# A Mamba-2 macaron block on 8 cores: the order of the in_proj columns, and the place of the SiLU gate

## The reference

```
x = x + 0.5 * ffn(layernorm(x))            # 1024 -> 4096 -> 1024, sin/cos transform and relu
x = x + attn(layernorm(x))                 # attn: its own layernorm, mamba2, residual, MLP with gelu
x = x + 0.5 * ffn(layernorm(x))
```

```python
zxbcdt = x @ in_proj_w.T                   # z: 2048, xBC: 2048 + 64 + 64, dt: 32
z, xBC, dt = split(zxbcdt)                 # dt = softplus(dt + dt_bias)
xBC = silu(conv1d_width_4(xBC) + conv_b)
# 32 heads of 64, state 64:  h = h*exp(dt*A) + dt*x*B ;  y = h.C + D*x
y = y * silu(z)                            # the gate
y = y * rsqrt(mean(y*y) + eps) * norm_w    # RMS norm over 2048
out = y @ out_proj_w.T
```

## Time and profile before

| | |
|---|---|
| time, median of 3 runs | 8764.91 us (8673.56, 8764.91, 8771.05) |
| the profiled execution | 8673.56 us |
| span of its slowest core (core 0) | 8671.6 us; the others 8571.8 to 8661.1 |
| busy share of the span | PE 61%, DVE 50%, ACT 22%, POOL 1% |
| mean DMA rate | 75 GB/s |

### The profile page before, as it was taken

How to read it: one execution, slowest core, us unless ns; L and a number is a source line. 1 busy time by engine, 2 the same in 40 slices (tenths; PEclk the granted TensorE clock), 3 DMA queues, 4 the chain that set the end, 5 groups by cost and what they waited for, 6 DMA issues and landing times.

```text
span 8671.6 us, 106339 instructions; the slowest of 8 cores (8571.8 to 8671.6 us)
## 1 busy us (share of the span) xinstructions
PE 5279.0 (61%) x22944; PEld 2303.2 (27%) x22944; DVE 4339.4 (50%) x11279; ACT 1874.3 (22%) x3876; POOL 60.1 (1%) x117
## 2 busy tenths in 40 slices
PE   0049999944544544445445344454468989888888
PEld 0013333322212222222222122222223434333333
DVE  2035656556456465565564655655632313556564
ACT  0022323221121211211212112112121222323232
POOL 2000000000000000000000000000000000000000
PEclk7568788865655755656557556566579999999999
DMA  9963333310100200101002001011024444343434
GB/s 171 204 155 116 107 117 117 110 50 1 40 29 1 67 1 9 59 1 37 31 1 67 1 7 61 1 35 33 1 81 136 136 134 139 112 136 117 137 123 129
DMA packets 191424, 652.87 MB, mean 75 GB/s; under 512 B 21472, under 2 KB 46176, under 8 KB 179552
## 3 DMA queue, kind: packets, MB, share of 16 engines
q1 hardware_dynamic: 174672, 590.41, 21.6%
q0 software_dynamic: 16176, 55.66, 4.4%
HBM read 629.56 MB, written 72.09 MB: 81 GB/s over the span
## 4 chain that ended last, share of the span: by engine, by line
PE 43%; DVE 31%; issue 13%; DMA 8%; ACT 3%; DVEq 2%; ACTq 0%; SPq 0%; POOL 0%; POOLq 0%
PE ps L252 42%; DVE arena L588 4%; DVE arena L583 4%; DVE arena L786 3%; DVE hstate L1045 3%; DVE arena L592 3%; DVE arena L939 3%; DVEq L92 2%; DVE arena L1124 2%; DMA arena<-wffn 2%; DMA arena<-wm 1%; DVE arena L995 1%; DMA cffn<-arena 1%; ACT arena L1109 1%; PE p L259 1%
## 5 line engine op out<-in xcount | busy, mean ns | idle before, releaser
L252 PE MATMUL ps<-arena,wk 128*128 128x512 f16 x15552 | 3710.1, 400 | 1004.9 <-DMA wk<-cffn 511.2
L252 PEld LDWEIGHTS ps<-arena,wk 128*128 128x128 f16 x15552 | 1554.5, 102 | 3152.7 <-issue 1880.0
L252 PE MATMUL ps<-arena 128*64 128x128 f16 (+1 forms) x1568 | 475.5, 303 | 1226.0 <-DVE arena L939 1162.7
L1061 ACT ACTIVATE arena<-arena 128x128 f32<-128x128 f32 x1024 | 316.6, 309 | 2197.4 <-DVE arena L995 2197.4
L583 DVE SCALAR_TENSOR_TENSOR arena<-arena,prm,ps 128x512 f32<-128x512 f32 x512 | 382.2, 746 | 647.4 <-ACT arena L581 559.1
L252 PEld LDWEIGHTS ps<-arena 128*64 128x64 f16 (+1 forms) x1568 | 198.3, 126 | 1467.8 <-issue 1404.4
L995 DVE TENSOR_SCALAR arena<-ps,arena 128x128 f32<-128x128 f32 x1024 | 358.9, 350 | 291.9 <-PE ps L252 217.3
L1004 DVE TENSOR_TENSOR arena<-arena,ps 64x128 f16<-64x128 f16 x1024 | 286.4, 280 | 387.0 <-PE ps L252 295.3
L578 ACT ACTIVATE arena<-ps,prm 128x512 f32<-128x512 f32 x512 | 352.0, 687 | 526.0 <-DVE arena L588 501.7
L252 PE MATMUL ps<-arena,ones 128*128 128x128 f16 (+1 forms) x832 | 250.3, 341 | 267.3 <-ACT arena L1109 141.4
L588 DVE SCALAR_TENSOR_TENSOR arena<-arena,prm 128x512 f32<-128x512 f32 x512 | 384.2, 750 | 54.7 <-DVE arena L583 1.8
(11 more groups left out here) (121 smaller groups left out, 3841.7 us busy)
## 6 DMA issues: line engine op xcount, KB each, us to landing
wk<-cffn SPq DMA_DIRECT2D x512, 512.0 KB, 4.0
wk<-cm SPq DMA_DIRECT2D x256, 512.0 KB, 3.7
wk<-cip SPq DMA_DIRECT2D x136, 512.0 KB, 3.6
wk<-cop SPq DMA_DIRECT2D x64, 512.0 KB, 3.8
arena<-wffn POOLq DMA_DIRECT2D x16, 1024.0 KB, 16.0
cffn<-arena SPq DMA_DIRECT2D x16, 1024.0 KB, 9.3
arena<-wm POOLq DMA_DIRECT2D x16, 1024.0 KB, 13.0
cm<-arena SPq DMA_DIRECT2D x16, 1024.0 KB, 6.9
```

What stands on the lines that cost most here:

```text
L252: e.matmul(a, l, r, start=st, stop=sp, tile_position=tp),
L1061: sD[s] = B.E("s", lambda e, s=s: e.activation(Dex[s % 2], e1[s % 2], AF.Exp), waits=[(s_v, ve1[s])], inc=s_s)
```

## The change

The in_proj loop runs over columns 0 to 34 in order, z first and dt last, and the weight units are queued in the same order. The gate of a pair of heads (128 features of `yq`) is done in the loop of slots, directly after that pair's L1033, with a wait for L1033's result and a wait for its own result behind it. The block of 16 gates in the tail is gone. Squares, ones-matmuls and everything else stay where they are in their engines' lists.

```diff
--- before.py
+++ after.py
@@ -726,16 +726,14 @@
                 B.E("v", lambda e, c=c: e.tensor_copy(
                     xbc[c][:, 0:3], sbar[:, c * 3:c * 3 + 3]), inc=s_v)
             B.dr("v")
-            uorder = list(range(8, 18)) + list(range(0, 8))
-            posmap = {ui: i for i, ui in enumerate(uorder)}
-            for ui in uorder:
+            for ui in range(nunit_ip):
                 w = 2048 if ui < 17 else 1024
                 stip.queue(ui * 2048, w)
             ip_evac = {}
             dt_done = None
-            for oc in list(range(16, 35)) + list(range(0, 16)):
+            for oc in range(35):
                 ui = oc // 2
-                sl, (sem, dv) = stip.unit(sc * nunit_ip + posmap[ui])
+                sl, (sem, dv) = stip.unit(sc * nunit_ip + ui)
                 boff = (oc % 2) * 1024
                 bank = oc % 4
                 for kc in range(8):
@@ -748,7 +746,7 @@
                          waits=w0, inc=(s_t if kc == 7 else None))
                 tmv = s_t.n
                 if oc % 2 == 1 or oc == 34:
-                    stip.consumed(sc * nunit_ip + posmap[ui], s_t, tmv)
+                    stip.consumed(sc * nunit_ip + ui, s_t, tmv)
                 if oc < 16:
                     sv = B.E("s", lambda e, b=bank, oc=oc: e.activation(
                         zsilu[:, oc * TT:(oc + 1) * TT], ps[b][:, 0:TT], AF.Silu),
@@ -876,6 +874,7 @@
                           waits=[(s_t, tmd)], inc=s_s)
                 guard(2, s_s, svA)
 
+                vgate = {}
                 tslot = {}
                 tD = {}
                 tTR = {}
@@ -1036,6 +1035,12 @@
                                 ALU.mult, ALU.add), waits=[(s_t, tY[hh])], inc=s_v)
                             vevac[2 * p2] = vevac[2 * p2 + 1] = vv
                             guard(ybk2, s_v, vv)
+                            vgate[p2] = B.E("v", lambda e, p2=p2, q=q: e.tensor_tensor(
+                                yq[:, p2 * 128:(p2 + 1) * 128],
+                                yq[:, p2 * 128:(p2 + 1) * 128],
+                                zsilu[:, p2 * TT + q * 128:p2 * TT + q * 128 + 128],
+                                ALU.mult), waits=[(s_v, vv)], inc=s_v)
+                            B.dr("v")
                         if hh % 2 == 1:
                             p = hh // 2
                             hbk = 2 + p % 2
@@ -1086,14 +1091,6 @@
                     gd(dbg[:, 10240:10240 + 2048], yq[:, :], waits=[(s_v, s_v.n)], inc=g_init)
                     B.W("v", [(g_init, g_init.n)])
                 B.dr("v")
-                vgate = {}
-                for c in range(NC16):
-                    vgate[c] = B.E("v", lambda e, c=c, q=q: e.tensor_tensor(
-                        yq[:, c * 128:(c + 1) * 128], yq[:, c * 128:(c + 1) * 128],
-                        zsilu[:, c * TT + q * 128:c * TT + q * 128 + 128], ALU.mult),
-                        waits=([(s_v, vevac[30]), (s_v, vevac[31])] if c == 0 else []),
-                        inc=s_v)
-                    B.dr("v")
                 if "dumpyn" in DBG_SKIP and q == 0 and sc == NTT - 1:
                     gd(dbg[:, 12288:12288 + 2048], yq[:, :], waits=[(s_v, s_v.n)], inc=g_init)
                     B.W("v", [(g_init, g_init.n)])
```

## The result

The changed kernel takes 9057.38 us (median of 12 runs, 8877.69 to 9219.33), the kernel before 8673.18 us (median of 14, 8580.08 to 8938.9). The ratio is 1.035 with a 95% interval of 1.0279 to 1.042: slower, by about 304 us on 8673. In some executions, the profiled one of the new kernel among them, part of the cores showed a lower granted clock and took longer; the ratio leaves those out and is therefore smaller than that of the medians (1.044).

A forecast was written before the change was run, and what follows sets the result against it. No engine is saturated overall (PE 61%); the head loop was taken as a serial chain with waits for DVE's own results. 310 - 86 + 47 = +271 us on 8765 gave 9036 us, range 8900 to 9110.

The forecast's parts named there:

- Part 1: Head loop on DVE: gate and its waits between L1033 and L1045 add 0.65 us a pair, +310 us.
- Part 2: Chunk tail: without the gates the first ones-matmul, Ln and next chunk come 2.7 us earlier, -86 us over 32 chunks.
- Part 3: in_proj to convolution: dt last delays L763, so conv 2 starts 5.92 us later, eight times, +47 us.
- (a): Rival for the head loop: gates hide in DVE's idle time, pair stays 4.90 us, sum -39, 8726 us; chance 0.07.
- (b): Rival for the head loop: waits are free, only operations cost, gate 108 us, sum +69, 8834 us; chance 0.06.
- (c): Rival for the in_proj order: convolution loses all its z cover, +225 us, sum +449, 9214 us; chance 0.04.
- (d): Rival for the tail: squares run inside the loop, 6 to 9 us saved a chunk, up to -241, 8524; chance 0.01.

The follow-up runs named there:

- e2: Only the gate moved into the loop, in_proj order of the kernel before; first to last tail Ln +242.3 us, median 8911.73 us beside 8761.38.
- e3: e2 without the wait for the gate's own result behind it; first to last tail Ln +106.7 us against the kernel before, median 8771.8 beside 8761.38.
- e5: Kernel before with each gate in the loop behind L995 of a later even slot, without a blocking wait; first to last Ln -68.1 us, median 8612.84 beside 8748.05.
- e1: Only the in_proj order changed, gate still in the tail; first to last tail Ln +41.9 us, median 8667.84 us beside 8761.38 of the kernel before.
- e8: Kernel before without five own-result waits per pair that the next DVE instruction doesn't need; first to last Ln -624.3 us, median 8148.78 beside 8748.05.

## Why the prediction was right

The forecast was +271 us, 9036 us; measured were 9057.38 us and a ratio of 1.035.

- **Part 1, the gate in the loop.** 0.65 us a pair was forecast, 0.90 us from L1033 to the state update; the trace has 0.90 and a pair 0.67 longer. e2 and e3 show it to be a link and a wait in a chain, and e5 that the same gate costs next to nothing outside the chain. 15 x 32 x 0.67 = 322 us instead of 310.
- **Part 2, the tail.** The mechanism was right and the size was off: -86 us forecast, about -70 measured. From the last L1033 to Ln it was to be 6.4 us, and it is 6.53. But the 9.09 us before came from the longest of the 32 chunks; all 32 have 8.62 to 9.09, with a mean of 8.76 and a median of 8.69. The second chunk (core 0, all engines) is typical:

```profile
2082.52 0.35 DVE L1033 SCALAR_TENSOR_TENSOR arena<-arena,prm,ps 128x128 f16<-128x128 f16 x1 [1.48 <-PE ps L252]
...
2084.94 0.39 PE L252 MATMUL ps<-arena,ones 128*128 128x128 f16 x2 [2.28 <-ACT arena L1109]
...
2091.19 0.37 ACT L1117 ACTIVATE arena<-ps,epsb 128x128 f32<-128x128 f32 x1 [0.51 <-PE ps L252]
```

It is 8.67 us here. By the means, 8.76 and 6.54, 2.2 us a chunk are saved, not 2.7, and the gain was put some 15 us too high. With the 12 us of part 1 that is the 27 us between the forecast sum, 271, and the two halves measured apart, 250 + 48 = 298.
- **Part 3, the order.** +47 us forecast, +48 measured by e1. 7.24 us from L763 to conv 2 were forecast, 7.25 found. A detail was wrong: the second table load doesn't follow Ln at once, it stands behind the wait for conv 0 (0.50 us idle), so the first Silu was ready 1.2 us ahead of conv 2, not 1.7. The cover held. A switch at the 2.66 us of the Trainium skill ("ScalarE: Activation LUTs", section "What ACT_TABLE_LOAD costs") isn't what this trace has: 1.30 us from the start of the load before the Silu to its ACTIVATE, as before the first z eviction of the old kernel.
- **The rivals.** (a) and (b) fall with e2 and e3, (c) with e1; (d) with the tail after, where the squares still lie behind the last pair. (The idle gaps of a pair in the earlier trace rows add up to 1.7 us and not to the 1.5 that stand in (a); nothing rests on it.) For (b), the rule of the Trainium skill ("VectorE: DVE Perf Modes", section "The DRAIN you can't avoid") that a semaphore after each operation costs nothing extra doesn't hold in this loop: e8 takes away nothing but waits and is 624 us shorter.
- **The base.** I put the sum on 8765, the median of three runs; 14 runs have 8673, the time of the profiled execution. On that base the forecast sum gives 8944, and the ratio of 1.035 gives 8977. That 9036 lies so near to 9057.38 is therefore partly luck: the loss was right within 12%, and the rest is the spread of the runs. The lower end of the range, 8900, is no result of the sum either: it takes 226 us, where the parts' low ends give 101 and the loop's alone 116. The range fitted, but the sum doesn't support its being so narrow below.

What stays open: why the same stretch is granted 0.78 on one core and 0.91 on another. No run here was made for that. Nor was any made that takes the five waits of e8 away one by one; their shares are known only from the gaps in the rows.

## What to carry to other kernels

Before an operation is moved "to where it is produced", look at what stands behind it on its engine: in this loop a link added to the chain cost its duration, the wait for its own result and the time of the waits behind that one, while beside the chain, in a gap that another engine causes, it cost next to nothing. A wait for an engine's own result belongs only in front of an instruction that reads it; in this loop five superfluous ones in a pair cost 1.2 of 5.0 us. And whether work is covered depends on the queue of every engine that it passes through: PE was busy and DVE free, but the Silus stood behind 16 evictions in ACT's queue.

## What the runs showed of the hardware

A wait on DVE for its own last result cost 0.10 us when it stood alone (the gates of the old tail start 0.32 us apart and take 0.225), and 0.24 us with two more waits behind it (L1050 after the change). It also took away the overlap of successive instructions, 0.05 us in e3 (L1040 and L1051) and 0.08 in e5 (L1002 and L895). Waits in front of the blocking one cost nothing in this row: L995 starts 0.11 us behind L939's end with four waits, the blocking one last. And the same in_proj takes 61 or 73 us on one core in one execution, by the granted clock: core 0 after the change, tile 1 and tile 7 (windows, columns as above; 270 and 273 matmul records). Neighbouring cores had the low clock in the same tiles: among the seven in_projs between the first and the last Ln, cores 0 and 1 in the first three, 6 and 7 in the first two, 2 and 3 in the last, and 4 and 5 for a part of the last.

```profile
1738.00:1812.00 74.00, 72.31 (x270) 29.77 (x271) 2.89 (x22) 21.62 (x35) 0.00 (x0) 0.79 0.41 125
5504.00:5565.50 61.50, 60.78 (x273) 27.12 (x273) 1.90 (x19) 21.62 (x35) 0.00 (x0) 0.96 0.49 150
```
